# Products that nobody reads in a decoder kernel's waits, and parts of a head group moved to a later place

## The reference, cut to what matters

```
x = x + attn0(norm(x))           # causal, 16 heads of 16, keys and values enhanced by a gated memory
x = x + xattn0(norm(x), ctx)     # 16 heads, rotary, causal mask, 154 keys
x = x + ffn0(norm(x))            # quantised linear 256->1024, depthwise conv, silu, quantised linear back
x = x + attn1(norm(x))           # 16 heads of 16, no mask
x = x + xattn1(norm(x), ctx)     # one wide head over 154 keys
x = x + moe(norm(x))             # 16 experts, top 2, and a shared one
```

## Time and profile before

| | |
|---|---|
| median of 3 runs | 3468.8 us (3467.74 to 3474.6) |
| profiled execution | 3478.01 us |
| its span, first to last instruction | 3476.7 us |
| TensorE busy | 3245.9 us, 93% |
| VectorE busy | 2332.4 us, 67% |
| ScalarE busy | 1787.6 us, 51% |
| GpSimdE busy | 565.4 us, 16% |
| mean granted TensorE clock | 0.950 of full speed |

### The profile page before, as it was taken

How to read it: one execution, slowest core, us unless ns; L and a number is a source line. 1 busy time by engine, 2 the same in 40 slices (tenths; PEclk the granted TensorE clock), 3 DMA queues, 4 the chain that set the end, 5 groups by cost and what they waited for, 6 DMA issues and landing times. The chain is left out here.

```text
span 3476.7 us, 46735 instructions
## 1 busy us (share of the span) xinstructions
PE 3245.9 (93%) x17684; PEld 1760.2 (51%) x17684; DVE 2332.4 (67%) x4331; ACT 1787.6 (51%) x2551; POOL 565.4 (16%) x1006
## 2 busy tenths in 40 slices
PE   5998979999999988999999988899999999899999
PEld 3544443368744443337864544333786444433477
DVE  4874578746685557865677557785667855788555
ACT  2464636653456454664344655466434555556632
POOL 0102010014111101002411120100241011020033
PEclk8899989999999998999998989899999999989999
DMA  3122011113121101201312120111131202012022
GB/s 133 38 38 43 2 28 28 20 41 117 40 47 35 38 1 28 38 10 62 117 35 40 26 38 1 37 29 33 60 102 40 38 16 38 1 37 38 10 80 94
DMA packets 118101, 147.74 MB, mean 42 GB/s; under 512 B 25384, under 2 KB 75920, under 8 KB 117596
## 3 DMA queue, kind: packets, MB, share of 16 engines
q1 hardware_dynamic: 117876, 144.74, 17.3%
HBM read 74.25 MB, written 4.46 MB: 23 GB/s over the span
## 5 line engine op out<-in xcount | busy, mean ns | idle before, releaser
L766 DVE TENSOR_REDUCE small<-psum 128x1 f32<-128x512 f32 (+6 forms) x1856 | 1147.7, 658 | 259.0 <-PE psum L621 217.3
L726 ACT ACTIVATE work<-psum 128x1024 f32<-128x1024 f32 (+5 forms) x1024 | 921.6, 935 | 453.8 <-PE psum L652 228.0
L621 PE MATMUL psum<-work 96*128 96x512 bf16 (+4 forms) x2688 | 698.9, 331 | 60.6 <-DMA work<-work 26.0
L1816 PE MATMUL psum<-rounded_work 128*128 128x512 f32 x2592 | 605.1, 395 | 9.9 <-DVE rounded_work L1902 6.5
L648 PE MATMUL psum<-work 99*128 99x512 bf16 (+4 forms) x2048 | 583.6, 369 | 9.3 <-DMA work<-work 8.1
L1816 PEld LDWEIGHTS psum<-rounded_work 128*128 128x128 f32 x2592 | 492.8, 191 | 116.2 <-DVE rounded_work L1902 8.3
L680 PE MATMUL psum<-work 128*32 128x512 f32 (+4 forms) x4480 | 534.9, 530 | 1.6 <-ACT work L726 1.4
L621 PEld LDWEIGHTS psum<-work 96*128 96x128 bf16 x2688 | 241.1, 102 | 578.7 <-DVE small L766 343.1
L648 PEld LDWEIGHTS psum<-work 99*128 99x128 bf16 (+1 forms) x2048 | 183.9, 99 | 201.1 <-ACT work L726 55.9
L1917 ACT CAST rounded_work<-work 128x512 fp32r<-128x512 f32 x144 | 89.4, 621 | 346.6 <-DVE work L1958 321.2
L808 POOL CAST small<-small 128x16 bf16<-128x16 f32 x96 | 18.8, 196 | 1297.6 <-issue 948.8
(11 more groups left out here) (291 smaller groups left out, 3934.7 us busy)
## 6 DMA issues: line engine op xcount, KB each, us to landing
work<-work SPq DMA_DIRECT2D x320, 192.0 KB, 4.3
work<-combine SPq DMA_DIRECT2D x64, 512.0 KB, 4.0
work<-in_w_gate SPq DMA_DIRECT2D x64, 128.0 KB, 3.5
work<-in_w_up SPq DMA_DIRECT2D x64, 128.0 KB, 3.5
work<-in_w_down SPq DMA_DIRECT2D x64, 128.0 KB, 3.7
work<-in_x SPq DMA_DIRECT2D x8, 512.0 KB, 5.5
out<-x SPq DMA_DIRECT2D x8, 512.0 KB, 2.9
work<-work SPq DMA_DIRECT2D x64, 28.9 KB, 2.0
```

The lines of the kernel that those rows point to most:

```text
L621: ins = nc.tensor.matmul(dst[:, c * n:(c + 1) * n], A.q_pair[0:ROWS, slot, h, P * i:P * (i + 1)], A.k_of(pair, h)[0:ROWS, s0:s0 + n], star ...
L726: nc.scalar.activation(probs[0:size, n % 4, :, 0:P * many], banks(2 * (n % 2), 2)[0:size, :, 0:P * many], ACT.Exp, scale=DH ** -0.5).then_ ...
L766: nc.vector.tensor_reduce(tops[:, pair % 2, places[0]:places[-1] + 1:step], src, AX.X, ALU.max) \
L1816: ins = nc.tensor.matmul(dst, a_parts[i], b_parts[j], start=start and n == 0, stop=stop and n == 2, skip_group_check=True)
```

## The change

It adds 110 products that nobody reads per trip: 6 ahead of the first unit of `own` and one behind each of its first 30 units; 6 ahead of `cross`, one behind each of its units 0 to 14 and ten behind unit 15; 14 ahead of `second`; and in the feed-forward 27 for 14, 20 for 12, and 8 new ones ahead of the wait for the hidden scale. In the attentions they go to bank 7, before anything is summed there. It moves the five late parts of the second group of heads in `own` from units 22 to 34 to units 42 to 54, and it spreads the eight value parts of `second` from every second unit to every fifth.

```diff
         heads = {A.tag: A for A in (Heads("own", FULL, True, 11, q_pair, slot_keys, V, [("context", n) for n in range(KD + 1)],
-                                          [(4, ("late", "gates", 0)), (22, ("late", "queries", 1)), (25, ("late", "rest", 2)), (28, ("late", "rest", 3)),
-                                           (31, ("late", "low", 2)), (34, ("late", "low", 3))]),
-                                    Heads("cross", CTX, True, 10, q_more_pairs, context_keys, V_ctx),
+                                          [(4, ("late", "gates", 0)), (42, ("late", "queries", 1)), (45, ("late", "rest", 2)), (48, ("late", "rest", 3)),
+                                           (51, ("late", "low", 2)), (54, ("late", "low", 3))] + [(n, ("fill", 1)) for n in range(30)]),
+                                    Heads("cross", CTX, True, 10, q_more_pairs, context_keys, V_ctx, (), [(n, ("fill", 1 if n < 15 else 10)) for n in range(16)]),
...
-                                          [(2 * i + 1, ("late", "values", i)) for i in range(NT)]))}
+                                          [(5 * i + 1, ("late", "values", i)) for i in range(NT)]))}
-        def heads_tensor(A, entered):
+        def heads_tensor(A, entered, wait):
             a, ring = A.tag, A.ring()
             entered(pe)
+            busy_tensor(wait, 7)
...
+                elif kind == "fill":
+                    busy_tensor(*key, 7)
...
         def feed_tensor():
-            busy_tensor(14)
+            busy_tensor(27)
             pe.wait_ge(*at("numbers_scaled"))
...
             pe.wait_ge(*at("convolved", NH - 2))
-            busy_tensor(12)
+            busy_tensor(20)
             pe.wait_ge(*at("activated", NH - 1))
...
             ins.then_inc(*up("tops_turned", 1))
+            busy_tensor(8)
             pe.wait_ge(*at("hidden_scale"))
...
-            heads_tensor(own_heads, gated_banks_free)
+            heads_tensor(own_heads, gated_banks_free, 6)
...
-            heads_tensor(cross_heads, cross_banks_free)
+            heads_tensor(cross_heads, cross_banks_free, 6)
...
-            heads_tensor(second_heads, second_banks_free)
+            heads_tensor(second_heads, second_banks_free, 14)
```

## The result

Over four runs each the kernel takes 3433.9 us (3428.0 to 3436.1) for 3468.4 (3467.7 to 3474.6): a ratio of 0.9894, with an interval of 0.9877 to 0.9911. The forecast was 3428 with a range of 3402 to 3462, on the side of faster. The profiled execution has a span of 3433.6 us; that of before had 3476.7, so the two profiles differ by 43.1, some 8 more than the medians (34.5).

What follows compares the result with a forecast made beforehand. TensorE was 93% busy at mean clock 0.950, with VectorE bounding the first units. Gains of 8.0 (`own`), 8.3 (`cross`), 4.8 and 7.4 (feed-forward) and 11.8 (`second`) sum to 40.3: 3468.8 - 40.3 = 3428.5 us, range 3402 to 3462.

Steps and rivals of the forecast that it cites:

- rivals 3 and 4: Low stretches lie where VectorE or a DMA bounds anyway: 3466, chance 0.08; clock falls all the same, slower: 3533, 0.07.
- the 5 named: Sign of being wrong: the third pair of `own` waits more than 5 us a trip.
- (f): Third pair of `own`: moved late parts load VectorE and make ScalarE wait for `rest`; cost 2.5 x 4 = 10 us.
- rival 2: `own`: (e) and (f) cost nothing, 16 us more gain, 3412; chance 0.14.
- rival 1: Moved parts in `own` are exposed: 10.8 us a trip, 33 more than in (f), 3461; chance 0.12.
- (a): `own`, first unit to first score: all four trips at the faster time, gates included; gain 2 x 4.2 = 8.4 us.
- (d): `own`: eight masked units with a product take 0.65, above VectorE's 0.56; cost 0.5 x 4 = 2 us.
- (e): `own`: clock falls again at the gates, then units pay 0.86 for 0.56; cost 1.5 x 4 = 6 us.
- (c): `own`, first scores: at 2.4 GHz bound by ScalarE's exponentials near 1.0 us a score; gain 1.6 x 4 = 6.4 us.
- (b): `own`: `queries 1` and one `rest` leave VectorE's time before the first score; gain 2.8 x 4 = 11.2 us.
- The 3.2 at stake: `second`: spread value parts keep the clock up to the first scores, 0.8 us a trip; by the skill page no gain.
- Rival 5: Whole kernel: all low time was waited for, half of 348 us comes back, 3295; chance 0.02.

Runs made afterwards that it cites:

- e1: The changed kernel with both moves undone and all added products kept: 3441.7 us, ratio 0.9908.
- e2: The kernel before with the two moves alone and none of the added products: 3452.3 us, ratio 0.9935.
- e7: e5 with 3 products for 6 ahead of `own` and 7 for 14 ahead of `second`: 3423.3 us, ratio 0.9859.
- e3: The changed kernel with the products added in the attentions 8 columns wide for 512, the feed-forward's kept at 512: 3436.5 us, ratio 0.9893.
- e5: The changed kernel without the 30 products beside the units of `own`: 3429.4 us, ratio 0.9875.
- e10: e5 with one product for ten behind unit 15 of `cross`: 3436.1 us, ratio 0.9902.
- e8: The changed kernel with the feed-forward's products as before (14, 12 and none ahead of the hidden scale): 3437.8 us, ratio 0.9899.

## Why the prediction was right, and where it was not

The mechanism was right: the products hold the clock (0.950 to 0.989, with the products alone 0.981, with the moves alone 0.967), which takes rivals 3 and 4 out. The third pair waits 2.2 us, below the 5 named; (f) cost 12.8 in all and neither nothing (rival 2) nor the 43 of rival 1. Term by term, from the profiles:

| term | forecast | measured | from |
|---|---|---|---|
| `own`, (a) gates, less (d) and (e) | -0.4 | -2.8 | first maximum to first exponential, e1 less before |
| `own`, (c) first scores | -6.4 | -3.9 | 1st to 13th exponential, e1 less before |
| `own`, entrance | 0 | +3.2 | e1 less before |
| `own`, (b) late parts out of the first units | -11.2 | -15.0 | after less e1 |
| `own`, (f) the same in the third pair | +10 | +12.8 | after less e1 |
| `cross` | -8.3 | -9.0 | after less before |
| feed-forward, turns | -4.8 | -7.4 | to the hidden top |
| feed-forward, scale | -7.4 | -6.5 | top to first scaled row |
| `second` | -11.8 | -13.1 | its three rows |

**`own`.** (a) alone was 8.4, and the gates gave 7.8. But e2, without a product, has 5.0 of them: before had slow gates in two trips, e2 in one. Trip 3, before and in e2:

```profile
1829.84 6.83 PE L997 MATMUL psum<-ident,work 128*128 128x8 f32 x32
```

```profile
1819.41 3.64 PE L997 MATMUL psum<-ident,work 128*128 128x8 f32 x32
```

After the change the clock fell behind the gates in trips 2, 3 and 4, as (e) had it; (d) and (e) together cost 4.5 in e1, for 8. **The entrance was forgotten**: six products between the last copy and the first unit were costed at nothing, since a wait stood there; the wait was for what the first unit needs too, and some 0.8 a trip is paid. With three for six (e7) it is 0.2, with six narrow ones (e3) 0.1. (b) and (f) were both sized too low, by 3.8 and 2.8, and nearly cancel; their sum, a gain of 1.2, measured 2.2. (c) was an estimate between 0 and 10.4 and came out at 1.0 a trip for 1.6. These single sizes are near the scatter of 4 us. What the sum hides: e5 and e2 reach as short an `own` (871.7 and 873.6 for 875.0) without unit products, e2 without any.

**`cross`** is the best of it: wait, number of products and pace of the scores came out, 5.92 for the 6.5 forecast, and e10 shows that it takes the ten in the wait.

**Feed-forward.** The size is right and half the reason: e8 gives 10.0 to its products, but e2 gains 9.2 with none. The same instructions, from the first maximum of the rows to the first scaled row, took 207.4 us in before, 203.4 in e8 and 198.2 in e2: where the clock is low there changes from one profile to the next. With the products they took 193.4 to 193.5 in all nine profiles that have them, so these are worth 5 to 14 by the execution that they are held against. What of it reaches the whole is not shown: e8 takes as long as the change.

**`second`.** First unit 1.40 later for 1.4, first score 2.55 earlier for 2.3. Of the 21.3 gained behind the first maximum the spread value parts alone give 8.5 + 4.9 (e2), the 14 products the rest, 7.9, for a price of 5.6. Not forecast: the projections ahead ran partly low in trips 2 and 4 too (for trip 1 the fifth stretch above has 0.83), so that the first maximum came 2.7 and 2.9 later there for 1.4.

The Trainium skill (TensorE: Matmul & The Clock Gate, HAM oscillation), which has the clock fall in long idle gaps, doesn't fit: before, the clock fell at 509.4 behind eight single units with a gap of 0.2 to 0.3 us before each. The last of them:

```profile
509.05 0.39 PE L621 MATMUL psum<-work 96*128 96x512 bf16 x1 [0.21 <-DVE small L766]
```

The spreading leaves gaps of the same length, but before two of each five units and no longer before each: in e2 TensorE is idle for 4.36 of 20 us and the clock keeps 1.00. The 3.2 at stake was won: 4.9.

**The step that failed** is the last one: 40.3 us, worked out against a profiled execution of 3478.0, were taken whole from a median of 3468.8. Against its own execution the sum is right to 2.8 us (43.1), in part by luck: 14.2 of these us (9.2 in the feed-forward, 5.0 at the gates) came in e2 without a product. Against the medians it is 34.5, by the ratio 36.8. A slow execution of before has more low time: of the 23 beside the experiments (3467.3 to 3480.1, median 3473.1) the seven up to 3470 have clocks of 0.954 to 0.956, the seven above 3475 of 0.950 to 0.952, and the profiled one has 0.950. So the sum gave back low stretches of which the median execution has fewer. That they lay where someone waits is argued, from e2's 9.2, and not shown. The 3468.8, from three executions, was itself 4 below the median of the 23.

**Rival 5** is refuted by size: low time fell by 272 us, half of which is 136, and 43 came back. The Trainium skill (TensorE: Matmul & The Clock Gate, Terms) counts the penalty as throttled time x (1 - K/N); here that is an upper bound, three times too high, since in most low stretches VectorE or a DMA was waited for (e5: clock 0.70, and no slower).

## What to carry to other kernels

Put unread products where TensorE waits for a DMA or a chain, as many as fit the wait, and where its next work is what others wait for; beside work that another engine bounds (the first units of `own`) they hold the clock and gain nothing that can be told. A move of real work, spread so that it fills the engine that starves, did the same in `second` with no product, and a late part is best put where the engine that carries it has slack, which is later than where the pressure begins. When a profiled execution is above the median, its low stretches can be partly luck: take that off before taking a gain from the median.

## What was unexpected of the hardware

- Among the units of `cross` TensorE was busy for 4.24 of 5.00 us with products of 8 columns and for 4.25 with products of 512, but the clock was 0.50 in the one (e3) and 1.00 in the other (e10).
- The clock can be low while TensorE is full. Two stretches of the third pair of `own` after the change, trip 1 (columns as above):

```profile
158.80:163.00 4.20, 3.12 (x28) 1.57 (x26) 3.16 (x7) 3.47 (x5) 0.00 (x0) 0.97 0.85 165
163.00:166.40 3.40, 3.40 (x15) 0.85 (x13) 2.64 (x6) 1.20 (x2) 0.00 (x0) 0.54 0.08 19
```

TensorE was busy for all of 3.40 us at the low clock; what came before the fall were its waits of 0.41 and 0.67, with 3.12 of 4.20 us busy. So two short waits in work that is otherwise full were followed by a fall in this trip, and by none in the other three. No product had been put into this pair, and none was tried there.
- Where the clock is low changes with the same code: 207.4, 203.4 and 198.2 us in the feed-forward of three profiles, and from the last fed row to `second` 24.6 or some 26.2 a trip within one. Whether work far ahead decides it or chance is not shown.
